# A selective-scan layer with experts on one core: the first half's out projection a state sooner, squares and norms in halves, the routing a state later

## The chip, the cores and the metric

The kernel runs on one core of a Trainium2 chip. The metric is the device time of one execution in microseconds (us), lower is better. The kernel before took 688.85 us (median of 3 runs, 685.72 to 689.6).

## The reference

The input is x of 4 sequences (batches) of 512 tokens, 128 wide. The program computes four residual steps; the change is in the first:

```
x = x + attn_a(layernorm(x))     # mamba block, then 8 experts, top 2
x = x + ffn(layernorm(x))
x = x + attn_b(layernorm(x))     # latent attention
x = x + ffn(layernorm(x))

attn_a(h0):
  h = rmsnorm(h0, w1);  xi, z = split(h @ in_proj)
  xi = silu(conv4(xi) + b)
  dbc = xi @ x_proj
  delta = softplus(dbc[:64] @ dt_proj + dt_b);  B = dbc[64:80];  C = dbc[80:96]
  for each of the 16 states n, over the 512 tokens t (256 channels):
     state_n[t] = exp(delta[t] * A_n) * state_n[t-1] + delta[t] * xi[t] * B_n[t]
     y[t] += state_n[t] * C_n[t]
  y = (y + D_skip * xi) * silu(z)
  r = h0 + y @ out_proj
  h2 = rmsnorm(r, w2)
  out = r + sum over the top 2 experts of weight * expert(h2)   # softmax of h2 @ router_w
```

## The kernel before, in words

Channels lie on the 128 partitions, so the 256 channels make two halves e = 0, 1, and tokens run along the free axis. One "state" g = 16 * b + n is state n of batch b; there are 64. `HB` = 2 batches make a half of the program: states 0 to 31 are the first half, states 32 to 63 the second; `first_1` = 32.

For each state five queues work:

- ScalarE (ACT): `decay(g, e)`, exp(delta * A_n) into PSUM (L1225). For states summed by VectorE it also copies the row of C into PSUM, `copy_c` (L1206), after the second decay. Further pieces of work are hung on (state, half) pairs by the table `COPY_AT` and run behind that decay: rows copied for the B and C store (`rows`, L1074), the softplus as `abs`, `relu`, `exp`, `log` (L1181, L1185, L1197, L1199), `squares` of r with their sums (L1068), `norm` (L1060), `input` (L1034), `logits` (L1048), `exps` (L1053). `c_by_token` (L1210) copies the turned C in state 35.
- GpSimd (POOL): the product delta * xi * B for both halves, called the B product here (L926, semaphore `dBx_ready`), into a ring of 3; for some states also the product of the scanned state with C, the C product (L935), two states later; the power for the second norm (`ROUTE_AT["power"]`, L887 and L888); `form_dx` (L914); and from state `SCATTER_FROM` = 48 on one of 16 scatters per state (`scatter`, L899), which put the first half's tokens into expert order.
- VectorE (DVE): the two scans of a state (L1574), for some states the weighing with C (L1586), `form_delta` (L1532), the gate of a finished batch (L1595), the residual additions (L1537), and the routing `top_a`, `top_b`, `find_slots` (L1446 to L1493).
- TensorE (PE): sums the weighed states with identity matmuls (`ysum`), projects ahead for the second half by the table `AHEAD`, runs `out_proj(0)` in state 34 ahead of that state's sums, and `turn_c` (L1953) in state 33, which turns the B and C rows for the states that are summed by token ("turned").
- SyncE (SP) issues the DMAs in program order: B row of state g (`spread_b`, L715), C row of state g - 2 (`spread_c`, L727), each spread to 128 partitions from a store in DRAM, and from state 36 on one of the 16 expert weights per state (L710). The first weight waits at L708 for `c_rows_turned`, since the weights land on memory that the first half used.

The order on each engine is written out by hand by these tables, and each queue runs in order. What the change touches is `AHEAD`, `COPY_AT`, `DELTA_AT`, `ROUTE_AT` and `SCATTER_FROM`, and the two helpers `norm_h2` and `squares`. What holds a queue shows in these lines:

```
if m == 0:                       # expert_weights, SyncE, state 36
    ...
    sp.wait_ge(s_ct, 1)
...
if AHEAD.get(g, ("",))[0] == "out_proj":    # PE, ahead of the sums
    ahead(*AHEAD[g])
...
sum_up(g - 1)
...
if g == TOKENS_AT:               # state 33
    turn_c()
...
if g == TOKENS_AT + 2:           # ACT, state 35
    c_by_token()
```

Of the kernel before, what the change touches and what calls it, by code (L numbers as in the profile page):

```python
# [36 lines left out]
def build(nc, x_in, rms1_w, rms2_w, in_proj_w, conv_w, conv_b, x_proj_w, dt_proj_w, dt_proj_b,  # L37
# [4 lines left out]
    TB = L // P  # L42
# [12 lines left out]
    HB = 2  # L55
# [9 lines left out]
    with ctx:  # L65
# [469 lines left out]
        for src, dst in ((0, wgT), (1, wuT), (2, None)):  # L535
            for t in range(HT):
# [18 lines left out]
                 16: ("taps", 1, 1), 18: ("taps1", 1, 0), 19: ("taps1", 1, 1), 22: ("x_proj", 0, 0), 24: ("dt_proj", 0, 0),  # L555
                 28: ("x_proj", 1, 0), 30: ("dt_proj", 1, 0), first_1 + 2: ("out_proj", 0, 0), 58: ("z", 1, 0), 61: ("z", 1, 1)}
        COPY_AT = {(5, 1): ("xi", 0, 0), (7, 1): ("xi", 0, 1), (9, 1): ("xi", 1, 0), (10, 1): ("xi", 1, 1),
                   (12, 1): ("conv", 0, 0), (13, 1): ("z", 0, 0), (15, 1): ("conv", 0, 1), (16, 1): ("z", 0, 1),
                   (21, 1): ("silu", 0, 0), (24, 1): ("rows", 0, 0), (26, 0): ("abs", 0, 0), (26, 1): ("relu", 0, 0),
                   (27, 0): ("abs", 0, 1), (27, 1): ("relu", 0, 1), (28, 0): ("exp", 0, 0), (29, 0): ("log", 0, 0),  # L560
                   (30, 1): ("rows", 1, 0), (32, 0): ("abs", 1, 0), (32, 1): ("relu", 1, 0), (33, 0): ("abs", 1, 1),
                   (33, 1): ("relu", 1, 1), (34, 0): ("exp", 1, 0), (35, 0): ("log", 1, 0),
                   (36, 0): ("squares", 0, 0), (36, 1): ("squares", 1, 0), (38, 0): ("norm", 0, 0), (38, 1): ("norm", 1, 0),
                   (40, 1): ("input", 0, 0), (41, 0): ("input", 1, 0), (43, 0): ("logits", 0, 0), (45, 0): ("exps", 0, 0),
                   (60, 1): ("z", 1, 0)}
        SILU_AT = 21
        XI_BANK, Z_BANK = ((5, 5), (5, 4)), ((4, 4), (4, 4))
        DELTA_AT = {4: 1, 30: 2, 36: 3}
        RESIDUAL_AT = first_1 + 3
        ROUTE_AT = {"power": first_1 + 6, "h2turn": first_1 + 7, "router": first_1 + 9,  # L570
                    "top_a": first_1 + 11, "top_b": first_1 + 13, "rank": first_1 + 14, "slots": first_1 + 15}
        TOKENS_AT = first_1 + 1
        SCATTER_FROM = first_1 + 16

# [438 lines left out]
        def _(act):  # L1013
# [40 lines left out]

            def norm_h2(c):

                act.wait_ge(s_rstd, 3)
                for j in range(TB):
                    t = TB * c + j
                    last = S.activation(nb[:, c, j, :], r[:, t, :], ACT.Copy, scale=small[:, 2, t:t + 1])  # L1060
                last.then_inc(s_h2, 1)

            def squares(c):

                act.wait_ge(s_r, c + 1)
                for j in range(TB):
                    t = TB * c + j
                    last = S.activation(nb[:, c, j, :], r[:, t, :], ACT.Square, accum_out=small[:, 3, t:t + 1])  # L1068
                if c == HB - 1:
                    last.then_inc(s_var, 1)  # L1070
# [90 lines left out]
            def copy_ahead(what, c, e):  # L1161
# [22 lines left out]
                elif what == "relu":  # L1184
                    S.activation(zr[:, e, L:HL], bank(DT[HB + c] + e), ACT.Relu, bias=dtb[:, e:e + 1]).then_inc(s_dtr, 1)  # L1185
                elif what == "squares":
                    squares(c)
                elif what == "norm":
                    norm_h2(c)
                elif what == "input":  # L1190
                    moe_input(c)
                elif what == "logits":
                    logits(0)
                elif what == "exps":
                    router_exp(0)
                elif what == "exp":
                    ch.link(S.activation(xT[:, :, :], xT[:, :, :], ACT.Exp, scale=-1.0))  # L1197
                elif what == "log":
                    S.activation(xT[:, :, :], xT[:, :, :], ACT.Ln, bias=1.0).then_inc(s_u, 1)  # L1199
# [1064 lines left out]
```

## Time and profile before

| | value |
|---|---|
| median of 3 runs | 688.85 us (685.72 to 689.6) |
| the profiled execution | 688.8 us, its span 687.0 us |
| PE busy | 570.7 us (83%) |
| VectorE busy | 475.6 us (69%) |
| ScalarE busy | 400.9 us (58%) |
| GpSimd busy | 324.6 us (47%) |
| scan, VectorE L1574 | 128 times, mean 1210 ns |
| B product, GpSimd L926 | 64 times, mean 2016 ns |
| C product, GpSimd L935 | 18 times, mean 2418 ns |
| decay, ScalarE L1225 | 128 times, mean 689 ns |
| chain that ended last | PE 36%, VectorE 9%, issue 7%, ScalarE 4%, GpSimd 3% |

The busy shares are averages over stages that have different limits. The states 0 to 63 run up to about 270 us; expert blocks, attention and feed-forward follow. What a change in one stage is worth is read from the timeline of that stage: each engine's rows in order of time, with the idle time before a row and what released it. Times in the rows count from the start of the span. In a matmul row one fp32 matmul stands as two records.

### The profile page before, as it was taken

What the parts mean: (1) busy time and instruction counts of PE and PEld (TensorE: products, weight loads), DVE (VectorE), ACT (ScalarE), POOL (GpSimd) and SP (SyncE); (2) the same over time, 40 slices, a digit from 0 to 9 for tenths busy, and PEclk for the clock granted to TensorE, in tenths of its full rate; (3) what the DMA queues carried; (4) which work ended last, traced back from release to release, by engine and by line L of the source; (5) the groups of instructions that cost most, each with busy time, mean ns of one, the idle gap of its engine ahead of it and who ended that gap; (6) DMA issues with size and microseconds to landing.
All of it is one profiled execution on the core that took longest, in us unless ns stands there. A gap on an engine that the chain in (4) does not pass through costs nothing.

```text
span 687.0 us, 11539 instructions
## 1 busy us (share of the span) xinstructions
PE 570.7 (83%) x3652; PEld 379.7 (55%) x3671; DVE 475.6 (69%) x1266; ACT 400.9 (58%) x666; POOL 324.6 (47%) x285
## 2 busy tenths in 40 slices
PE   2967899678677887889989999757799989988887
PEld 1423343224254564879989899625545545544466
DVE  4759997998789987536335653587777878886052
ACT  2677657756755776556756656314356556656731
POOL 5259988895996994225785324412011112112010
PEclk9979999899897999999999999957999999999999
DMA  5845455443755453201152003232003003000001
GB/s 142 305 167 159 150 186 154 143 129 109 241 183 160 142 135 100 68 16 36 54 133 86 20 17 105 68 100 58 9 25 87 10 20 92 4 3 3 1 16 47
DMA packets 49085, 63.32 MB, mean 92 GB/s; under 512 B 7570, under 2 KB 29090, under 8 KB 48770
## 3 DMA queue, kind: packets, MB, share of 16 engines
q1 hardware_dynamic: 43682, 56.65, 27.5%
q0 software_dynamic: 2496, 5.15, 2.1%
q10 hardware_dynamic: 2848, 0.78, 0.5%
q8 instruction: 31, 0.51, 0.3%
q14 instruction: 28, 0.23, 0.1%
HBM read 44.84 MB, written 9.52 MB: 79 GB/s over the span
## 4 chain that ended last, share of the span: by engine, by line
PE 36%; DVE 9%; issue 7%; ACT 4%; POOL 3%; DMA 1%; ACTq 1%; POOLq 0%; another core or an unknown queue 0%; DVEq 0%
PE ps L1792 33%; DVE arena L1712 3%; ACT arena L1296 2%; POOL moe_rows L899 1%; DVE stats L1383 1%; PE ps L2153 1%; DVE x L1647 1%; POOL moe_out L907 1%; DVE nb L1396 1%; ACT r L1296 1%; DMA moe_out<-arena,xT 1%; PE ps L2160 1%; ACT arena L1316 1%; ACT arena L1304 1%; ACTq L1286 1%
## 5 line engine op out<-in xcount | busy, mean ns | idle before, releaser
L1792 PE MATMUL ps<-arena 128*128 128x128 f32 (+11 forms) x2147 | 329.2, 329 | 42.9 <-DVE arena L1712 17.9
L1792 PEld LDWEIGHTS ps<-arena 128*128 128x128 f32 (+2 forms) x2166 | 209.0, 157 | 130.2 <-issue 59.3
L1574 DVE TENSOR_TENSOR_SCAN arena<-ps,arena 128x512 f32<-128x512 f32 x128 | 149.8, 1210 | 21.4 <-ACT ps L1225 15.2
L926 POOL TENSOR_TENSOR arena<-arena 128x1024 f32<-128x1024 f32 x64 | 127.9, 2016 | 25.5 <-DVE arena L1561 19.8
L1792 PE MATMUL ps<-arena,ident 128*128 128x512 f32 x216 | 109.5, 644 | 30.9 <-DVE arena L1586 30.8
L1712 DVE CUSTOM_DVE_ANT_0 arena<-ps,cmask 128x128 f32<-128x128 f32 (+3 forms) x256 | 111.5, 488 | 26.4 <-PE ps L1792 25.2
L1225 ACT ACTIVATE ps<-arena 128x512 f32<-128x512 f32 x128 | 87.4, 689 | 47.2 <-DVE arena L1574 45.5
L1792 PEld LDWEIGHTS ps<-arena,ident 128*128 128x128 f32 x216 | 42.4, 207 | 85.9 <-issue 44.2
L1296 ACT ACTIVATE arena<-ps 128x1024 f32<-128x1024 f32 (+3 forms) x86 | 57.0, 709 | 38.0 <-PE ps L1792 37.6
L907 POOL DMA_INDIRECT moe_out<-arena,xT x46 | 44.9, 976 | 66.5 <-DVE arena L1736 57.1
L1766 DVE TENSOR_TENSOR arena<-arena,ps 128x512 f32<-128x512 f32 x46 | 31.6, 688 | 57.1 <-PE ps L1792 43.6
L1343 ACT COPY arena<-arena 128x1024 f32 x46 | 48.2, 1048 | 13.9 <-issue 13.9
L871 POOL TENSOR_TENSOR small<-small,neghalf 128x4 f32<-128x4 f32 (+1 forms) x13 | 14.0, 1074 | 89.2 <-DVE small L1663 73.8
L935 POOL TENSOR_TENSOR arena<-arena 128x1024 f32<-128x1024 f32 x18 | 43.5, 2418 | 14.2 <-DVE arena L1574 13.1
L1353 ACT ACTIVATE arena<-ps 128x512 f32<-128x512 f32 x52 | 31.1, 598 | 24.4 <-PE ps L1792 22.3
L1586 DVE TENSOR_TENSOR arena<-arena,ps 128x1024 f32<-128x1024 f32 x36 | 43.1, 1198 | 0.2
L899 POOL DMA_INDIRECT moe_rows<-nb,xT x32 | 32.3, 1008 | 15.6 <-DVE xT L1493 8.6
L968 POOL TENSOR_TENSOR x<-x,arena 128x128 f32<-128x128 f32 x16 | 7.4, 460 | 67.4 <-DVE arena L1725 67.2
L1296 ACT ACTIVATE r<-ps 128x512 f32<-128x512 f32 (+3 forms) x42 | 27.8, 701 | 16.9 <-PE ps L1792 16.5
L1792 PE MATMUL ps<-kmask,identb 128*128 128x128 bf16 x256 | 35.1, 219 | 0.0
L1746 DVE TENSOR_TENSOR arena<-arena,ps 128x512 f32<-128x512 f32 x18 | 12.3, 686 | 28.7 <-ACT arena L1316 28.5
L1792 PEld LDWEIGHTS ps<-kmask,identb 128*128 128x128 bf16 x256 | 23.7, 98 | 12.4
(220 smaller groups left out, 700.3 us busy)
## 6 DMA issues: line engine op xcount, KB each, us to landing
arena<-bc_rows SPq DMA_DIRECT2D x118, 256.0 KB, 3.7
arena<-arena SPq DMA_DIRECT2D x64, 64.0 KB
arena<-arena SPq DMA_DIRECT2D x28, 128.0 KB, 2.4
moe_rows<-arena SPq DMA_DIRECT2D x2, 1495.0 KB, 11.8
arena<-moe_rows SPq DMA_DIRECT2D x8, 325.0 KB, 4.3
arena<-in_L_attn_a_Wg SPq DMA_DIRECT2D x8, 256.0 KB, 4.2
arena<-in_L_attn_a_Wu SPq DMA_DIRECT2D x8, 256.0 KB, 4.8
arena<-moe_out SPq DMA_DIRECT2D x4, 512.0 KB, 4.5
```

Of the source, the lines that this page charges most:

```text
L899: G.indirect_dma_start(moe_rows[h], bass.IndirectOffsetOnAxis(ap=slotu[:, h, k, t:t + 1], axis=0), nbr[:, t // TB, t % TB, :], None).then_ ...
L907: G.indirect_dma_start(moe_out[h], bass.IndirectOffsetOnAxis(ap=target[:, h, k:k + 1], axis=0), yb[:, i % YR, :], None).then_inc(s_yst[i % ...
L926: G.tensor_tensor(dBx[:, g % RING, :, :], dx[:, :, cs], bs[:, g % BS, :].unsqueeze(1).to_broadcast([P, CT, L]), ALU.mult).then_inc(s_dbx, 1)
L935: G.tensor_tensor(hC[:, slot(p), :, :], hst[:, p % STATES, :, :], cs_rows[:, row_slot(p), :].unsqueeze(1).to_broadcast([P, CT, L]), ALU.mu ...
L1225: S.activation(bank(6 + e), delta[:, e, c * L:c * L + L], ACT.Exp, scale=aneg[:, e, n:n + 1]).then_inc(s_da, 1)
L1296: S.activation(pts[c % 3][:, 2 * q:2 * q + 2, kt * P:L], ps[:, 2 * q:2 * q + 2, kt * P:L], ACT.Exp).then_inc(s_ex, 1)
L1343: S.copy(wst[:, i % 2, :, :].rearrange("p g f -> p (g f)"), wgu[:, bass.ds(expert, 1), :, :].rearrange("p o g f -> p (o g f)")).then_inc(s ...
L1574: V.tensor_tensor_scan(hst[:, g % STATES, e, :], bank(6 + e), dBx[:, g % RING, e, :], 0.0, ALU.mult, ALU.add).then_inc(s_scan, 1)
L1586: V.tensor_tensor(hC[:, slot(g), :, :], hst[:, g % STATES, :, :], bank(c_bank(g)).unsqueeze(1).to_broadcast([P, CT, L]), ALU.mult).then_in ...
L1712: last = V.tensor_tensor_reduce(out=junk[:, m % 2, col:col + w], in0=ps[:, 4 + m % 2, col:col + w], in1=cmask[:, L - w:L], scale=-1.0, sca ...
L1766: V.tensor_tensor(hs[:, i % 2, :], sg[:, m % 2, :], bank(2 + m % 2), ALU.mult).then_inc(s_hm, 1)
L1792: return T.matmul(o, l, rr, start=start, stop=stop)
```

## The change

The out projection of the first half runs on PE in state 33 rather than 34. The last batch's softplus runs on ScalarE a state sooner (`rows` at state 29 ... `log` at 34), but `form_delta(3)` on VectorE goes from state 36 to 38. `squares` and `norm` take half a batch (two tiles of 128 tokens) at a time, in four places each rather than two: squares in states 36 and 37, norms in 39 and 40 (before: 36, and 38). The power, the turn of h2, the router, `top_a`, `top_b`, the ranks and the slots, and the first scatter, all come one state later. No instruction is added or removed but the split of the loops.

```diff
-                 28: ("x_proj", 1, 0), 30: ("dt_proj", 1, 0), first_1 + 2: ("out_proj", 0, 0), 58: ("z", 1, 0), 61: ("z", 1, 1)}
+                 28: ("x_proj", 1, 0), 30: ("dt_proj", 1, 0), first_1 + 1: ("out_proj", 0, 0), 58: ("z", 1, 0), 61: ("z", 1, 1)}
...
-                   (30, 1): ("rows", 1, 0), (32, 0): ("abs", 1, 0), (32, 1): ("relu", 1, 0), (33, 0): ("abs", 1, 1),
-                   (33, 1): ("relu", 1, 1), (34, 0): ("exp", 1, 0), (35, 0): ("log", 1, 0),
-                   (36, 0): ("squares", 0, 0), (36, 1): ("squares", 1, 0), (38, 0): ("norm", 0, 0), (38, 1): ("norm", 1, 0),
-                   (40, 1): ("input", 0, 0), (41, 0): ("input", 1, 0), (43, 0): ("logits", 0, 0), (45, 0): ("exps", 0, 0),
+                   (29, 1): ("rows", 1, 0), (31, 0): ("abs", 1, 0), (31, 1): ("relu", 1, 0), (32, 0): ("abs", 1, 1),
+                   (32, 1): ("relu", 1, 1), (33, 0): ("exp", 1, 0), (34, 0): ("log", 1, 0),
+                   (36, 0): ("squares", 0, 0), (36, 1): ("squares", 0, 1), (37, 0): ("squares", 1, 0), (37, 1): ("squares", 1, 1),
+                   (39, 0): ("norm", 0, 0), (39, 1): ("norm", 0, 1), (40, 0): ("norm", 1, 0), (40, 1): ("norm", 1, 1),
+                   (41, 1): ("input", 0, 0), (42, 0): ("input", 1, 0), (43, 1): ("logits", 0, 0), (46, 0): ("exps", 0, 0),
...
-        DELTA_AT = {4: 1, 30: 2, 36: 3}
+        DELTA_AT = {4: 1, 30: 2, 38: 3}
...
-        ROUTE_AT = {"power": first_1 + 6, "h2turn": first_1 + 7, "router": first_1 + 9,
-                    "top_a": first_1 + 11, "top_b": first_1 + 13, "rank": first_1 + 14, "slots": first_1 + 15}
+        ROUTE_AT = {"power": first_1 + 7, "h2turn": first_1 + 8, "router": first_1 + 10,
+                    "top_a": first_1 + 12, "top_b": first_1 + 14, "rank": first_1 + 15, "slots": first_1 + 16}
...
-        SCATTER_FROM = first_1 + 16
+        SCATTER_FROM = first_1 + 17
...
-            def squares(c):
+            def squares(c, half):
...
-                for j in range(TB):
+                for j in range(2 * half, 2 * half + 2):
...
-                if c == HB - 1:
+                if half and c == HB - 1:
                     last.then_inc(s_var, 1)
```

`norm_h2` is cut in the same way; its semaphore is raised in the second half alone.

How the order of instructions moves is shown at three places. First PE in state 33, the turn of the C rows (L1953, `turn_c`) and the out projection (the rows 128x128). Before:

```order
L1792 MATMUL ps<-arena 128x512 [waits y_gated]
L1792 MATMUL ps<-arena 128x512
L1792 MATMUL ps<-arena,ident 128x512 [waits hC_ready]
L1792 MATMUL ps<-arena,ident 128x512
L1953 MATMUL ps<-ident,arena 128x32 [waits hC_ready,dt_ready]
L1953 MATMUL ps<-ident,arena 128x32 x7
L1792 MATMUL ps<-arena 128x128 [waits y_gated,dt_product_read]
L1792 MATMUL ps<-arena 128x128 x15
```

and with the change:

```order
L1794 MATMUL ps<-arena 128x512 [waits y_gated]
L1794 MATMUL ps<-arena 128x512
L1794 MATMUL ps<-arena 128x128 [waits y_gated,dt_product_read]
L1794 MATMUL ps<-arena 128x128 x15
L1794 MATMUL ps<-arena,ident 128x512 [waits hC_ready]
L1794 MATMUL ps<-arena,ident 128x512
L1955 MATMUL ps<-ident,arena 128x32 [waits hC_ready,dt_ready]
L1955 MATMUL ps<-ident,arena 128x32 x7
```

The out projection has moved ahead of the sum of state 32 and of the turn of the C rows.

Second ScalarE from the copy of the turned C (state 35) to the first decay of state 38. L1225 are the decays, L1206 the copies of a C row, L1068 the squares. Before:

```order
L1210 COPY arena<-ps 128x256 [waits c_rows_turned]
L1225 ACTIVATE ps<-arena 128x512 [waits scan_done]
L1068 ACTIVATE nb,small<-r 128x128 [waits residual_ready]
L1068 ACTIVATE nb,small<-r 128x128 x3
L1225 ACTIVATE ps<-arena 128x512 [waits scan_done]
L1206 COPY ps<-arena 128x512 [waits hC_ready,c_row_spread0]
L1068 ACTIVATE nb,small<-r 128x128 [waits residual_ready]
L1068 ACTIVATE nb,small<-r 128x128 x3
L1225 ACTIVATE ps<-arena 128x512 [waits scan_done] x2
L1206 COPY ps<-arena 128x512 [waits hC_ready,c_row_spread1]
L1225 ACTIVATE ps<-arena 128x512 [waits scan_done]
```

and with the change:

```order
L1212 COPY arena<-ps 128x256 [waits c_rows_turned]
L1227 ACTIVATE ps<-arena 128x512 [waits scan_done]
L1070 ACTIVATE nb,small<-r 128x128 [waits residual_ready]
L1070 ACTIVATE nb,small<-r 128x128
L1227 ACTIVATE ps<-arena 128x512 [waits scan_done]
L1208 COPY ps<-arena 128x512 [waits hC_ready,c_row_spread0]
L1070 ACTIVATE nb,small<-r 128x128 [waits residual_ready]
L1070 ACTIVATE nb,small<-r 128x128
L1227 ACTIVATE ps<-arena 128x512 [waits scan_done]
L1070 ACTIVATE nb,small<-r 128x128 [waits residual_ready]
L1070 ACTIVATE nb,small<-r 128x128
```

followed by

```order
L1227 ACTIVATE ps<-arena 128x512 [waits scan_done]
L1208 COPY ps<-arena 128x512 [waits hC_ready,c_row_spread1]
L1070 ACTIVATE nb,small<-r 128x128 [waits residual_ready]
L1070 ACTIVATE nb,small<-r 128x128
L1227 ACTIVATE ps<-arena 128x512 [waits scan_done] x3
```

The squares are spread over four places; the last two now stand between the copy of C row 37 and the decay of state 38.

Third VectorE from the second scan of state 36 on, with `form_delta(3)` (L1532). Before:

```order
L1574 SCALAR_TENSOR_TENSOR arena<-ps,arena 128x512 [waits dA_ready]
L1532 TENSOR_TENSOR arena<-arena,xT 128x2x512 [waits softplus_log_ready]
L1574 SCALAR_TENSOR_TENSOR arena<-ps,arena 128x512 [waits hC_ready,dBx_ready,dA_ready]
L1586 TENSOR_TENSOR arena<-arena,ps 128x1024 [waits y_summed,scan_done,c_row_copied]
L1574 SCALAR_TENSOR_TENSOR arena<-ps,arena 128x512 [waits dA_ready]
```

and with the change, from the same scan:

```order
L1576 SCALAR_TENSOR_TENSOR arena<-ps,arena 128x512 [waits dA_ready]
L1576 SCALAR_TENSOR_TENSOR arena<-ps,arena 128x512 [waits hC_ready,dBx_ready,dA_ready]
L1588 TENSOR_TENSOR arena<-arena,ps 128x1024 [waits y_summed,scan_done,c_row_copied]
L1576 SCALAR_TENSOR_TENSOR arena<-ps,arena 128x512 [waits dA_ready]
L1576 SCALAR_TENSOR_TENSOR arena<-ps,arena 128x512 [waits hC_on_pool_ready,dBx_ready,dA_ready]
L1588 TENSOR_TENSOR arena<-arena,ps 128x1024 [waits y_summed,scan_done,c_row_copied]
L1576 SCALAR_TENSOR_TENSOR arena<-ps,arena 128x512 [waits dA_ready]
L1534 TENSOR_TENSOR arena<-arena,xT 128x2x512 [waits softplus_log_ready]
```

`form_delta(3)` stands two states further on, behind the second scan of state 38. (The rows name a scan SCALAR_TENSOR_TENSOR; the trace names it TENSOR_TENSOR_SCAN.)

## Rows read from the trace of the kernel before

**Rows 1.** Chain of waits, one piece of it (start, us, what)

```profile
276.18 0.11 PE ps L2032
```

**Rows 2.** Busy time of one stretch: PE, PEld, DVE, ACT, POOL, granted clock, DMA, GB/s

```profile
217.00:266.00 49.00, 40.86 (x222) 27.65 (x221) 44.39 (x40) 34.80 (x71) 46.05 (x31) 1.00 0.42 128
```

**Rows 3.** DVE by time: start, us, line, operation, [idle before <- releaser]

```profile
143.51 3.18 DVE L1532 TENSOR_TENSOR arena<-arena,xT 128x1024 f32<-128x1024 f32 x1
...
167.08 0.69 DVE L1537 TENSOR_TENSOR r<-ps,r 128x512 f32<-128x512 f32 x1 [2.50 <-PE ps L1792]
...
169.47 2.33 DVE L1574 TENSOR_TENSOR_SCAN arena<-ps,arena 128x512 f32<-128x512 f32 x2
...
171.72 1.20 DVE L1532 TENSOR_TENSOR arena<-arena,xT 128x1024 f32<-128x1024 f32 x1
...
176.07 1.22 DVE L1574 TENSOR_TENSOR_SCAN arena<-ps,arena 128x512 f32<-128x512 f32 x1 [3.15 <-ACT ps L1225]
...
179.74 1.22 DVE L1574 TENSOR_TENSOR_SCAN arena<-ps,arena 128x512 f32<-128x512 f32 x1 [0.20 <-ACT ps L1225]
...
202.51 1.22 DVE L1574 TENSOR_TENSOR_SCAN arena<-ps,arena 128x512 f32<-128x512 f32 x1 [2.03 <-issue]
...
216.52 0.17 DVE L1493 CAST xT<-xT 128x16 uint32<-128x16 f32 x1
```

**Rows 4.** PE by time

```profile
161.58 2.87 PE L1792 MATMUL ps<-arena,ident 128*128 128x512 f32 x4
...
164.38 0.68 PE L1953 MATMUL ps<-ident,arena 32*128 32x32 f32 x8
...
164.99 3.84 PE L1792 MATMUL ps<-arena 128*128 128x128 f32 x32
...
168.66 3.60 PE L1792 MATMUL ps<-arena,ident 128*128 128x512 f32 x8
...
209.68 1.94 PE L1967 MATMUL ps<-ident,arena 128*128 128x128 f32 x8 [7.31 <-DVE arena L1574]
```

**Rows 5.** One microsecond, 163 to 164; columns as in rows 2

```profile
163.00:164.00 1.00, 1.00 (x3) 0.33 (x1) 1.00 (x2) 0.60 (x2) 1.00 (x1) 0.72 0.00 0
```

**Rows 6.** Waits of SyncE's DMA queue (us in total, times, longest)

```profile
SPq L708 <- PE ps L1953: 11.0, 1, 11.0
```

**Rows 7.** DMA issues of SyncE's queue by time

```profile
167.44 0.43 SPq L727 DMA_DIRECT2D arena<-bc_rows  x1
```

**Rows 8.** The source line L727 (C rows), 150 to 182 us

```profile
DMA to landing us min/median/max: 3.5/4.4/6.7
```

**Rows 9.** ACT by time

```profile
165.09 0.37 ACT L1210 COPY arena<-ps 128x256 f32<-128x256 f32 x1 [1.50 <-PE ps L1953]
...
173.66 0.59 ACT L1206 COPY ps<-arena 128x512 f32<-128x512 f32 x1 [4.00 <-DMA arena<-bc_rows]
...
174.18 0.30 ACT L1068 ACTIVATE nb<-r 128x128 f32<-128x128 f32 x1
...
175.36 1.28 ACT L1225 ACTIVATE ps<-arena 128x512 f32<-128x512 f32 x2
```

**Rows 10.** POOL by time, up to 225 us

```profile
169.74 2.00 POOL L926 TENSOR_TENSOR arena<-arena 128x1024 f32<-128x1024 f32 x1 [5.16 <-DMA arena<-bc_rows]
...
171.69 3.43 POOL L935 TENSOR_TENSOR arena<-arena 128x1024 f32<-128x1024 f32 x1
...
189.56 2.36 POOL L935 TENSOR_TENSOR arena<-arena 128x1024 f32<-128x1024 f32 x1
```

**Rows 11.** POOL by time, from 217 us

```profile
217.00 1.23 POOL L899 DMA_INDIRECT moe_rows<-nb,xT  x1 [6.42 <-DVE xT L1493]
...
263.27 2.01 POOL L926 TENSOR_TENSOR arena<-arena 128x1024 f32<-128x1024 f32 x1
```

**Rows 12.** SyncE's queue by time, from 262 us

```profile
267.79 11.81 SPq L757 DMA_DIRECT2D arena<-moe_rows  x5
```

More of the change, by code:

```diff
@@ L1053, in router_exp, with norm_h2 @@
                 S.activation(wtok[:, tiles_of(h), :], wtok[:, tiles_of(h), :], ACT.Exp).then_inc(s_re, 1)
-            def norm_h2(c):
+            def norm_h2(c, half):
                 act.wait_ge(s_rstd, 3)
-                for j in range(TB):
+                for j in range(2 * half, 2 * half + 2):
                     t = TB * c + j
                     last = S.activation(nb[:, c, j, :], r[:, t, :], ACT.Copy, scale=small[:, 2, t:t + 1])
-                last.then_inc(s_h2, 1)
-            def squares(c):
+                if half:
+                    last.then_inc(s_h2, 1)
+            def squares(c, half):
                 act.wait_ge(s_r, c + 1)
-                for j in range(TB):
+                for j in range(2 * half, 2 * half + 2):
                     t = TB * c + j
                     last = S.activation(nb[:, c, j, :], r[:, t, :], ACT.Square, accum_out=small[:, 3, t:t + 1])
-                if c == HB - 1:
+                if half and c == HB - 1:
                     last.then_inc(s_var, 1)
@@ L1186, in copy_ahead @@
                 elif what == "squares":
-                    squares(c)
+                    squares(c, e)
                 elif what == "norm":
-                    norm_h2(c)
+                    norm_h2(c, e)
                 elif what == "input":
```

## The prediction, made before the changed kernel ran

> **What bounds the kernel now.** I read the chain of waits first. It shows pieces only from 268 us on, and there it is serial: last sums, gate, second out projection, and the turn of the first expert block at 276.18 [rows 1]. So whatever the end of the scans loses or wins is passed on to the end of the kernel. Then the busy time by stretch, to see who paces the scans. From 217 to 266 us POOL is busy 46.05 of 49 us [rows 2]. Its own timeline says the same: from the first scatter at 217.00 to the product with B of state 63 that ends at 265.28 it repeats a scatter and a product, 16 scatters and 15 products, 15 steps of 3.21 us and a start of its own [rows 11]. VectorE is not the limit there; it is the end of `find_slots` at 216.69 [rows 3] that starts this row of work. So the question is what the change does to the time at which the slots are ready, and how much POOL has done by then.
>
> Between 159 and 217 us I followed VectorE's timeline for its holes. There are four that count [rows 3]: 2.50 us before the first residual addition at 167.08 (it waits for the out projection), 3.15 us before the scan of state 37 at 176.07, 0.20 us before state 38, and 2.03 us before state 45 at 202.51. The second is the one to understand. The scan waits for a decay of ScalarE at 175.36, which stands behind the second batch's four squares (from 174.18) and the copy of C row 36 at 173.66, and that copy waited 4.00 us for a DMA [rows 9]. The row was issued only at 167.44 [rows 7]. It was late because SyncE's queue stood still for 11.0 us at L708, the first expert weight, until PE had turned the C rows at L1953 [rows 6]. POOL felt it as well: its product for state 37 waited 5.16 us for a B row [rows 10]. So the turn of the C rows (`turn_c`, at 164.38 [rows 4]) is what releases the row traffic.
>
> **The change, part by part.**
>
> *Out projection ahead.* On PE it moves from behind `turn_c` to ahead of the sum of state 32. It starts at 161.58 instead of 164.99 [rows 4]. PE is then at half clock: in 163 to 164 us the granted clock averages 0.72 [rows 5], so 0.56 us of it were at 1.2 GHz (0.5 x 0.56 + 0.44 = 0.72) and 2.4 GHz came back at 163.56. A 128x128 record costs (168.66 - 164.99)/32 = 0.115 us at full clock and about 1.94/8 = 0.24 at 1.2 GHz [rows 4]. Of the 32 records some 8 run in the slow 2.0 us, the other 24 take 2.8, so it ends at 166.3. The sum of state 32 follows with four records of 0.43 (eight took 3.60 [rows 4]), 1.7 us, and `turn_c` starts at 168.0, **3.6 us later**. Bounds: all at full clock, 161.58 + 3.7 + 1.7 = 167.0 (+2.6); all at half clock, 161.58 + 7.7 + 2.9 = 172.1 (+7.7). I take 3.6, since the clock's history up to 161.58 is unchanged.
>
> *What it gives.* The 2.50 us hole before 167.08 closes. But ScalarE's copy of the turned C (at 165.09, behind a wait for L1953 [rows 9]) now comes at 168.7, and the decay of state 36 stands behind it. The scan of state 36 therefore starts at about 169.6, where it started at 169.47 [rows 3]. The gain is zero.
>
> *What it costs.* SyncE is released 3.6 us later, and issues the same transfers in the same order. C row 36 lands at 177.2 instead of 173.66, B row 37 at 173.3. ScalarE's copy, two squares (half of the 1.18 us from 174.18 to 175.36 [rows 9]) and the decay follow, so the scan of state 37 starts 3.6 - 0.6 = 3.0 us later, at 179.1. The 0.6 comes back at once: the last two squares now stand between the copy of C row 37 and the decay of state 38. State 38 is **+3.6 us**, at 183.3.
>
> *Last softplus a state sooner.* All of it sits on ScalarE before 163 us beside scans that don't wait for it; `abs` at state 31 stands behind `form_delta` (ends 146.69 [rows 3]) and still ahead of the decay that needs the scan of state 30. Its cover is that wait. The last `relu`, which the out projection waits for, comes before the gate that it waits for too. 0 us.
>
> *`form_delta(3)` from state 36 to 38.* It took 1.20 us at 171.72 [rows 3], inside the hole that ended at 176.07, so it was free. Behind the second scan of state 38 nothing hides it: **+1.1 us** for VectorE. At the same moment POOL starts the C product of state 38. When the two met at 171.7, POOL's product took 3.43 us against 2.36 alone [rows 10], so POOL pays 1.07 too. It has the slack of a wait for the scan of state 40 for part of it: the C product of state 40, at 189.56 before, comes at 194.1, **+4.5 us** in all (VectorE alone would make it +4.0).
>
> Which side pays depends on who is first. In the other order VectorE paid: 3.18 us at 143.51 [rows 3], 2.0 us more than 1.20, which would make the scan of state 40 5.9 us late.
> The Trainium skill, page "SBUF — State Buffer", section "Who interferes with whom", has it that a VectorE instruction with two SBUF inputs and a GpSimd instruction that reads SBUF exclude each other, the first to issue holding the shared ports to its end; that rule speaks against this move, which takes `form_delta` to where a product starts, and the trace shows both orders of it.
>
> *Norms and power.* POOL's power (about 1.9 us) moves behind the product of state 39. It starts when the last square is read, about 182.7, and the B product of state 40 ends about 186.6, just as the scan of state 38 does: no cost, but without margin. The norms end in state 40, and PE turns them then; nobody waits on PE.
>
> *To state 45.* From the C product of state 40 on, POOL was busy without a hole up to the scan of state 45: 202.51 - 189.56 = 12.95 us [rows 3, 10], and the change adds nothing to POOL there. State 45 comes at 207.0, still +4.5. The first routing piece (2 us) moves into the wait before it, which gives nothing, as it is POOL that ends that wait.
>
> *Routing a state later.* The slots now end after two more scans and one weighing: 3 x 1.12 = 3.4 us. In return POOL makes the product of state 49 before it waits for the slots, and so has one step of 3.21 us less to do after them [rows 11]. Net +0.2. One scatter more stands behind the last product. The gathered rows, loaded from 267.79 [rows 12], would be asked for at 273.5, and PE needs them at 280.9 (276.18 + 4.7); landing takes about 4 us by the nearest row I have (3.5 to 6.7 [rows 8]), so it stays hidden.
>
> **Sum.** +4.5 + 0.2 = +4.7 us on the profiled execution's 688.8, **693.5 us**. The median of the three runs shown is 688.85, so the two bases agree.
>
> **The rivals.** A measurement of this kernel can tell about 0.5% (3.4 us) from no change.
>
> (A) *The row comes faster.* C row 36 took 6.2 us from issue to use; other C rows landed after 4.4, at best 3.5 [rows 8]. If the shifted transfers meet less traffic and the row lands after 3.5, the copy starts at 174.5, +0.9, and the end is +0.9 + 0.9 + 0.2, about 690.8 us: not slower. Against it: the same ten transfers are issued within the same 5 us, so they crowd each other as before. It decides from a landing under 4.9 us.
>
> (B) *Half clock.* If PE stays at 1.2 GHz through the out projection, `turn_c` is 7.7 us late rather than 3.6, and the time is 697.6. For it: that half clock ended at 163.56 just as the work changed; against it: PE is busy without a hole in both.
>
> (C) *VectorE loses the port*, see above: 5.9 + 0.2, 694.9 us.
>
> (D) *Nothing is late.* If the rows did not hang on `turn_c`, the holes of 2.50 and 3.15 would both close; with 0.6 for the squares before state 38, 1.1 for `form_delta` and 0.2 behind, -5.65 + 1.9 = -3.7, 685.1 us. The 11.0 us at L708 [rows 6] speaks against it.
>
> **How the numbers follow.** The forecast 0.55, A 0.20, B 0.08, C 0.09, D 0.05, and 0.03 for the change having no effect at all. Slower by over 0.5% are B, C and most of the forecast's own spread (692 to 695; a tenth falls under 692.3): 0.66. Faster is D with a little of A: 0.06. The same takes the rest, 0.28. The range of 8 in 10 goes from 688.5, inside A, to 696.5, between C and B; the forecast's own bounds are 692.0 (both lock costs gone, `turn_c` at +2.6) and 695.
>
> **What would show it.** Right, if in the new profile `turn_c` starts at about 168 behind the out projection; L708 waits 14 to 15 us; the copy of C row 36 starts near 177; a hole of about 2.6 us stands before state 36 and one of about 7 us before the scan of state 37, near 179; `find_slots` ends near 224.5; and the last scan starts near 270.5. The hole before the residual addition gone, and the one before state 37 more than twice its 3.15 us, is the mark of the mechanism. Wrong, if the copy of row 36 starts before 175 (A), or if the time from state 38 to the slots is not that of before.

## The result, and the profile after

| | before | after |
|---|---|---|
| median | 688.67 us (685.72 to 689.6, 4 runs) | 694.36 us (693.61 to 696.57, 4 runs) |
| the profiled execution | 688.8 us, span 687.0 us | 693.63 us, span 691.9 us |
| first gate to third gate, VectorE | 157.78 to 272.85: 115.07 us | 158.76 to 276.71: 117.95 us |
| third gate to the end of the span | 414.15 us | 415.19 us |

The kernel became slower: ratio 1.0089, interval [1.0056, 1.0122], in microseconds +3.9 to +8.4. But for the softplus of the last batch, all that the change moves lies between the gate of batch 1 and the gate of batch 3 (L1595 before, L1597 after; the first and the third gate from 150 us on, and so called below). The third line of the table is where its effect must be read. There the profiled execution lost 2.9 us, less than the medians say; why is answered below. The profiled execution after reaches its first gate 0.98 us later than that of before; these 0.98 us are there in full at the first scan of state 28 already (136.81 and 137.79), ahead of everything that the change moves. Wherever times of two executions are compared, they are therefore counted from the first gate.

The rows of after follow the order of the prediction. PE by time (start, us, line, operation; the 36 records at 160.03 are 4 of the skip product and the 32 of the out projection):

```profile
160.03 5.55 PE L1794 MATMUL ps<-arena 128*128 128x512 f32 x36 [1.83 <-DVE arena L1597]
...
165.43 1.89 PE L1794 MATMUL ps<-arena,ident 128*128 128x512 f32 x4
...
167.24 0.68 PE L1955 MATMUL ps<-ident,arena 32*128 32x32 f32 x8
```

The turn of the C rows (L1955) has moved behind the out projection and the sum of state 32. It starts 8.48 us after the first gate, before 6.60 [rows 4]: 1.88 us later. SyncE's wait at the first expert weight grew with it, from 11.0 us [rows 6] to 12.9:

```profile
SPq L709 <- PE ps L1955: 12.9, 1, 12.9
```

SyncE's queue by time: the queue starts again 0.8 us behind the turn, and C row 36 is issued 2.3 us later, as before in the same order (167.44 there [rows 7]):

```profile
168.01 0.34 SPq L711 DMA_DIRECT2D arena<-in_L_attn_a_Wg  x1
...
170.29 0.43 SPq L728 DMA_DIRECT2D arena<-bc_rows  x1
```

ScalarE by time, for [rows 9]:

```profile
167.95 0.37 ACT L1212 COPY arena<-ps 128x256 f32<-128x256 f32 x1 [3.89 <-PE ps L1955]
...
176.37 0.59 ACT L1208 COPY ps<-arena 128x512 f32<-128x512 f32 x1 [6.27 <-DMA arena<-bc_rows]
...
176.90 0.30 ACT L1070 ACTIVATE nb<-r 128x128 f32<-128x128 f32 x1
...
177.49 0.67 ACT L1227 ACTIVATE ps<-arena 128x512 f32<-128x512 f32 x1
...
181.14 0.30 ACT L1070 ACTIVATE nb<-r 128x128 f32<-128x128 f32 x1
```

The copy of the turned C waits 3.89 us for PE, and the copy of C row 36 waits 6.27 us for its DMA (before: 1.50 and 4.00). Row 36 is used 6.08 us after its issue, before 6.22 [rows 7, 9]: it did not come faster, it was asked for later. VectorE by time, for [rows 3]:

```profile
158.76 1.22 DVE L1597 TENSOR_TENSOR arena<-ps,arena 128x1024 f32<-128x1024 f32 x1
...
165.48 0.69 DVE L1539 TENSOR_TENSOR r<-ps,r 128x512 f32<-128x512 f32 x1
...
167.21 0.67 DVE L1539 TENSOR_TENSOR r<-ps,r 128x512 f32<-128x512 f32 x1
...
168.95 2.41 DVE L1576 TENSOR_TENSOR_SCAN arena<-ps,arena 128x512 f32<-128x512 f32 x2 [1.07 <-ACT ps L1227]
...
178.19 1.22 DVE L1576 TENSOR_TENSOR_SCAN arena<-ps,arena 128x512 f32<-128x512 f32 x1 [6.83 <-ACT ps L1227]
...
182.44 1.22 DVE L1576 TENSOR_TENSOR_SCAN arena<-ps,arena 128x512 f32<-128x512 f32 x1 [0.78 <-ACT ps L1227]
...
185.83 1.20 DVE L1534 TENSOR_TENSOR arena<-arena,xT 128x1024 f32<-128x1024 f32 x1
...
206.05 3.45 DVE L1576 TENSOR_TENSOR_SCAN arena<-ps,arena 128x512 f32<-128x512 f32 x3 [1.96 <-POOL arena L927]
...
223.67 0.17 DVE L1495 CAST xT<-xT 128x16 uint32<-128x16 f32 x1
...
269.68 1.23 DVE L1576 TENSOR_TENSOR_SCAN arena<-ps,arena 128x512 f32<-128x512 f32 x1 [0.20 <-ACT ps L1227]
...
276.71 1.22 DVE L1597 TENSOR_TENSOR arena<-ps,arena 128x1024 f32<-128x1024 f32 x1 [2.25 <-PE ps L1794]
```

The hole of 2.50 us before the first residual addition is gone, the one before the scan of state 37 has grown from 3.15 to 6.83 us, a hole of 1.07 us stands before state 36, and `form_delta(3)` sits at 185.83 with no idle time around it. Last GpSimd by time, for [rows 10, 11]:

```profile
172.59 2.00 POOL L927 TENSOR_TENSOR arena<-arena 128x1024 f32<-128x1024 f32 x1 [7.04 <-DMA arena<-bc_rows]
...
181.92 0.19 POOL L888 TENSOR_SCALAR small<-small 128x8 f32<-128x8 f32 x1 [1.13 <-ACT nb L1070]
...
186.04 3.20 POOL L936 TENSOR_TENSOR arena<-arena 128x1024 f32<-128x1024 f32 x1 [0.25 <-DVE arena L1576]
...
193.12 2.36 POOL L936 TENSOR_TENSOR arena<-arena 128x1024 f32<-128x1024 f32 x1
...
224.15 1.23 POOL L900 DMA_INDIRECT moe_rows<-nb,xT  x1 [7.82 <-DVE xT L1495]
...
267.12 2.01 POOL L927 TENSOR_TENSOR arena<-arena 128x1024 f32<-128x1024 f32 x1
```

The B product of state 37 waits 7.04 us for its row (before 5.16). The product of state 38 starts 0.21 us behind `form_delta` and takes 3.20 us where one alone takes 2.36. The first scatter comes at 224.15 with 14 products behind it where before had 15 [rows 11], and the last of them ends at 269.1.

One thing was not expected. These are two windows of before, from 160 us on (PE, weight load, VectorE, ScalarE, GpSimd busy; granted clock; DMA share; GB/s):

```profile
160.00:162.00 2.00, 2.00 (x4) 0.86 (x3) 2.00 (x3) 1.78 (x4) 1.74 (x1) 0.54 0.00 0
162.00:164.00 2.00, 2.00 (x4) 0.66 (x2) 2.00 (x3) 1.60 (x3) 2.00 (x2) 0.61 0.00 0
```

and the same of after:

```profile
160.00:162.00 2.00, 1.97 (x6) 1.01 (x7) 2.00 (x2) 0.86 (x2) 0.76 (x1) 1.00 0.00 0
162.00:164.00 2.00, 2.00 (x21) 2.00 (x20) 2.00 (x3) 1.59 (x3) 2.00 (x2) 1.00 0.00 0
```

Before ran here at 1.2 GHz for most of the time, after at 2.4 GHz throughout. The out projection, which the prediction had start at half clock, ran at full clock.

### The profile page after: what moved, and what is told of

Read it like the earlier page. It is cut to its first block, busy times and chain, and to the rows that moved or that the text cites. A ratio compares the mean times of both kernels' runs of the same rounds, so it can differ in the third digit from the quotient of the medians.

```text
span 691.9 us, 11558 instructions
## 1 busy us (share of the span) xinstructions
PE 574.8 (83%) x3671; PEld 380.5 (55%) x3671; DVE 475.3 (69%) x1266; ACT 400.2 (58%) x666; POOL 323.9 (47%) x285
## 4 chain that ended last, share of the span: by engine, by line
PE 36%; DVE 9%; issue 7%; ACT 4%; POOL 3%; DMA 1%; ACTq 1%; POOLq 0%; DVEq 0%
PE ps L1794 33%; DVE arena L1714 3%; ACT arena L1298 2%; POOL moe_rows L900 1%; DVE stats L1385 1%; PE ps L2155 1%; DVE x L1649 1%; POOL moe_out L908 1%; DVE nb L1398 1%; PE ps L2162 1%; DMA moe_out<-arena,xT 1%; ACT arena L1318 1%; ACTq L1288 1%; DVE mv L1388 0%; ACT arena L1306 0%
## 5 line engine op out<-in xcount | busy, mean ns | idle before, releaser
L1794 PE MATMUL ps<-arena 128*128 128x128 f32 (+11 forms) x2166 | 333.0, 329 | 44.2 <-DVE arena L1714 17.9
L1576 DVE TENSOR_TENSOR_SCAN arena<-ps,arena 128x512 f32<-128x512 f32 x128 | 150.0, 1210 | 27.3 <-ACT ps L1227 21.3
L1208 ACT COPY ps<-arena 128x512 f32<-128x512 f32 x36 | 20.9, 580 | 17.0 <-DMA arena<-bc_rows 10.0
```

Of the source, the lines that this page charges most:

```text
L1576: V.tensor_tensor_scan(hst[:, g % STATES, e, :], bank(6 + e), dBx[:, g % RING, e, :], 0.0, ALU.mult, ALU.add).then_inc(s_scan, 1)
L1794: return T.matmul(o, l, rr, start=start, stop=stop)
```

## The experiments

Ten kernels ran, in three groups, each group on one chip together with the kernel before. On the chip of the first and third group every kernel takes some 11 us more (before: 699.57 and 700.46 us), on that of the second group before took 689.03 us. Ratios are always to the runs of before on the same chip.

All readings of the profiled executions stand in one table; times in us from the first gate (VectorE L1595, with the change L1597). "Clock" is PE's level there: half where the two windows above average 0.50 to 0.59 and 0.55 to 0.97, full where both are 1.00. "Slots" is the start of `find_slots`' last instruction.

| kernel | clock | first gate at | turn of C | copy of C row 36 | slots | third gate |
|---|---|---|---|---|---|---|
| before | half | 157.78 | 6.60 | 15.88 | 58.74 | 115.07 |
| after | full | 158.76 | 8.48 | 17.61 | 64.91 | 117.95 |
| after, again | full | 158.57 | 8.48 | 17.65 | 65.00 | 118.11 |
| out projection only | full | 158.10 | 8.49 | 17.49 | 60.34 | 116.59 |
| all but the out projection | full | 159.58 | 4.91 | 14.64 | 61.97 | 115.08 |
| turn early in before | half | 158.01 | -0.75 | 11.02 | 56.23 | 112.56 |
| turn early in after | half | 157.39 | -0.80 | 9.56 | 58.24 | 111.29 |
| `form_delta` at 38 only | half | 156.52 | 6.60 | 16.09 | 59.80 | 116.12 |
| after, `form_delta` at 36 | half | 157.37 | 10.14 | 18.97 | 65.46 | 118.57 |
| out projection and turn early | half | 156.67 | -0.90 | 9.34 | 54.65 | 110.89 |
| routing only | half | 156.78 | 6.60 | 15.37 | 61.84 | 114.88 |
| turn early, `form_delta` at 36 | full | 158.29 | -0.62 | 9.24 | 58.68 | 111.77 |

### The out projection alone, and all but it

The first kernel is before with only this:

```diff
-  first_1 + 2: ("out_proj", 0, 0)
+  first_1 + 1: ("out_proj", 0, 0)
```

> The kernel before with the out projection alone moved to state 33. Theory (the turn of the C rows stands behind it and holds the row traffic): the turn starts 1.9 us (full clock, as in the profile of the change) to 3.6 us (half clock first) later, L708 waits 13 to 15 us, the scan of state 37 and all behind it come 1.9 to 3.6 us later, so the ratio to before is 1.003 to 1.005. Rival (it is the rest of the change that costs, and the earlier out projection gives 2.5 us by the hole before the residual addition): 0.996 to 0.999.

Measured: 702.98 us against 699.57, ratio 1.0064 [1.0044, 1.0084], a little above the 1.003 to 1.005 that was expected. The turn stood 8.49 us behind the gate, and SyncE waited 12.9 us at the first weight. The second is after with the same line put back:

```diff
-  first_1 + 1: ("out_proj", 0, 0)
+  first_1 + 2: ("out_proj", 0, 0)
```

> The changed kernel with the out projection put back to state 34: squares and norms in halves, softplus sooner, form_delta at 38, routing later. Theory: the C row of state 36 is copied near 173.7 as before, the halves of the squares cancel, form_delta costs about 1 us and the routing 0.2, ratio to before 1.001 to 1.003. Rival (the rest is what costs): 1.006 or more.

Measured: 700.88 us, ratio 1.0019 [1.0002, 1.0035]. So the loss is in the out projection's move, and the rest costs a little: added, the two ratios give 1.0083. VectorE of the second kernel, for the two holes in question:

```profile
167.18 0.69 DVE L1539 TENSOR_TENSOR r<-ps,r 128x512 f32<-128x512 f32 x1 [0.79 <-PE ps L1794]
...
176.04 1.22 DVE L1576 TENSOR_TENSOR_SCAN arena<-ps,arena 128x512 f32<-128x512 f32 x1 [4.14 <-ACT ps L1227]
```

With the out projection behind the turn, the hole before the residual addition is back (0.79 us at full clock, 2.50 at half), and that before state 37 is 4.14 us rather than 6.83. The second kernel and after ran at the same clock. From gate to gate they differ by 117.95 - 115.08 = 2.87 us, with the turn 8.48 - 4.91 = 3.57 us later. Most of the missing 0.7 us is the row: from the turn to the copy of C row 36 it took 17.61 - 8.48 = 9.13 us in after and 14.64 - 4.91 = 9.73 in the second kernel.

### The turn of the C rows ahead of it all

If everything hangs on when PE turns the C rows, then turning them a state sooner must win, whatever the out projection does. In before and in after:

```diff
-        TOKENS_AT = first_1 + 1
+        TOKENS_AT = first_1
```

> The kernel before with the turn of the C rows on PE in state 32 and its copy on ScalarE in state 34. Theory: SyncE is released near 157 instead of 165, no engine waits for a row in states 36 and 37, the hole of 3.15 us before the scan of state 37 goes and that of 2.50 stays, the scan of state 37 starts near 173, ratio to before 0.995 to 0.996. Rival (the row is late for its own traffic, not for SyncE's wait): the copy of C row 36 still starts after 172 and the ratio is 0.999 to 1.001.

Measured: 697.53 us, ratio 0.9974 [0.9959, 0.9989]: faster, by less than was expected. The hole before the residual addition stays (1.59 us), and `form_delta(3)` took 2.71 us beside a product of GpSimd.

> The changed kernel with the turn of the C rows in state 32 and its copy in state 34, so that the out projection has nothing of the row traffic behind it. Theory: the holes of 1.07 and 6.83 us before states 36 and 37 go, the scan of state 37 starts near 170.5, ratio to before 0.995 to 0.998, some 7 to 8 us under the changed kernel, and near or under the kernel with the early turn alone. Rival (the change costs by other parts): ratio to before over 1.000.

Measured: 695.82 us, ratio 0.9955 [0.994, 0.9971], so it is faster than before while after is slower. No hole is left before states 36 and 37. From gate to gate the changed kernel falls from 117.95 us (full clock) to 111.29 us (half clock) by this one line. The two kernels with the early turn ran at the same level, and between them the rest of the change loses nothing any more: 111.29 us against 112.56. So what the change costs is not the work it moves but the turn that it delays.

### `form_delta` and its place

```diff
-        DELTA_AT = {4: 1, 30: 2, 36: 3}
+        DELTA_AT = {4: 1, 30: 2, 38: 3}
```

> The kernel before with form_delta of the last batch moved from state 36 to 38 alone. Theory: 1.0 to 1.2 us more on the way to the slots, gate to gate 116.1 us against 115.1, ratio 1.001 to 1.003. Rival (no cost): 0.999 to 1.001 and 115.1.

Measured, this line alone in before: 689.26 us against 689.03, ratio 1.0012 [0.9985, 1.0038]. The time does not tell it from nothing; from gate to gate, at the same clock as before, it is 116.12 - 115.07 = 1.05 us. Of these 16.09 - 15.88 = 0.21 us are a C row that came later, which leaves 0.84 us for `form_delta`. The opposite edit in after:

> The changed kernel with form_delta of the last batch back in state 36, inside the hole of 6.8 us. Theory (it costs where it was put, on VectorE and by GpSimd's product beside it): 1 to 2 us less than the changed kernel, ratio to before 1.004 to 1.007, gate to gate 116 to 117 us. Rival (GpSimd ends the later waits and has the slack): no difference from the changed kernel.

Measured: 692.95 us, ratio 1.0064 [1.0039, 1.0088]. From gate to gate it took 118.57 us and not the 116 to 117 expected, but at half clock, with the turn 10.14 - 8.48 = 1.66 us later than in after; less these it would be 116.9 us, an estimate. After itself ran beside it:

> The changed kernel as it is, once more beside before, on the chip of the runs it is compared with. If the parts add up, out projection (1.0064) and rest (1.0019) give 1.008; a ratio of 1.006 to 1.010 is expected. From gate to gate (start of the gate of batch 1 to that of batch 3) 117.9 us as in the first profile, against 115.1 before.

Measured: 693.53 us, ratio 1.0056 [1.003, 1.0083], just under the 1.006 to 1.010 expected, and 118.11 us from gate to gate. By the time the two can't be told apart. The first of them is worth more for another reason: it is the changed order of PE in an execution with half clock. PE by time:

```profile
158.65 7.22 PE L1794 MATMUL ps<-arena 128*128 128x512 f32 x36 [1.98 <-DVE arena L1597]
...
165.70 1.89 PE L1794 MATMUL ps<-arena,ident 128*128 128x512 f32 x4
...
167.51 0.68 PE L1955 MATMUL ps<-ident,arena 32*128 32x32 f32 x8
```

The same 36 records take 7.22 us here and 5.55 in after. VectorE of the same kernel:

```profile
169.22 2.41 DVE L1576 TENSOR_TENSOR_SCAN arena<-ps,arena 128x512 f32<-128x512 f32 x2 [2.63 <-ACT ps L1227]
...
171.55 1.20 DVE L1534 TENSOR_TENSOR arena<-arena,xT 128x1024 f32<-128x1024 f32 x1
...
178.16 1.22 DVE L1576 TENSOR_TENSOR_SCAN arena<-ps,arena 128x512 f32<-128x512 f32 x1 [5.41 <-ACT ps L1227]
```

The hole before state 36 is 2.63 us, as the prediction gave it (2.6), and 1.07 in after at full clock.

### The routing alone

This is before with the routing and the first scatter a state later, and with the pieces that stand between them on ScalarE; norms, squares, power, `form_delta` and the out projection stay:

```diff
-  (40, 1): ("input", 0, 0), (41, 0): ("input", 1, 0), (43, 0): ("logits", 0, 0), (45, 0): ("exps", 0, 0),
+  (41, 1): ("input", 0, 0), (42, 0): ("input", 1, 0), (43, 1): ("logits", 0, 0), (46, 0): ("exps", 0, 0),
...
-  ROUTE_AT = {"power": first_1 + 6, "h2turn": first_1 + 7, "router": first_1 + 9,
-              "top_a": first_1 + 11, "top_b": first_1 + 13, "rank": first_1 + 14, "slots": first_1 + 15}
+  ROUTE_AT = {"power": first_1 + 6, "h2turn": first_1 + 8, "router": first_1 + 10,
+              "top_a": first_1 + 12, "top_b": first_1 + 14, "rank": first_1 + 15, "slots": first_1 + 16}
...
-  SCATTER_FROM = first_1 + 16
+  SCATTER_FROM = first_1 + 17
```

> Only the routing of the kernel before goes a state later: the turn of h2, the router, top_a, top_b, the ranks and the slots, with the norms' inputs, logits and exps behind them, and the first scatter in state 49; the power stays in state 38, the out projection in 34, form_delta in 36. Theory (the term of the prediction): two scans and one weighing more stand ahead of the slots (+3.4 us), and GpSimd has one step of 3.21 us less to do after them, so from the first gate to the third it takes 115.1 to 115.6 us where the kernel before took 115.07 with its PE at half clock at the turn of the C rows; with PE at full clock there both are about 1.7 us less. Ratio to the kernel before 0.999 to 1.002. Rival: GpSimd's head start is lost again (it does not pace the states behind the slots by itself), then 118.3 us and 1.004 to 1.006. Second rival: the slots themselves come less than 3.4 us later because two holes of VectorE fill, then below 115 us.

Measured: 700.48 us against 700.46, ratio 0.9987 [0.9963, 1.0011], and 114.88 us from gate to gate, 0.2 less than before at the same clock. The slots are ready 61.84 - 58.74 = 3.10 us later, yet the third gate is not. C row 36 was in use 0.51 us sooner in this execution; without that the routing would cost 0.51 - 0.19 = 0.3 us, so the head start of GpSimd makes up for nearly all of the later slots, and the rival with 118.3 us is out. GpSimd of this kernel, first scatter and the product behind it:

```profile
219.10 1.23 POOL L899 DMA_INDIRECT moe_rows<-nb,xT  x1 [7.81 <-DVE xT L1493]
...
220.37 2.00 POOL L926 TENSOR_TENSOR arena<-arena 128x1024 f32<-128x1024 f32 x1
```

### A version that beats both

The out projection of the change, the turn a state sooner, and nothing else, in before:

```diff
-  first_1 + 2: ("out_proj", 0, 0)
+  first_1 + 1: ("out_proj", 0, 0)
...
-        TOKENS_AT = first_1 + 1
+        TOKENS_AT = first_1
```

> The kernel before with two edits: turn of the C rows in state 32 (copy in 34) and out projection in state 33. Theory: nothing hangs on the out projection then, so the hole of 2.50 us closes as well and it gains on the early turn alone (0.9974): ratio 0.993 to 0.996, gate to gate 110.5 to 112. Rival (GpSimd already ends every wait there): the same as the early turn alone, 0.996 to 0.998.

Measured: 683.86 us (681.18 to 686.11) against 689.03, ratio 0.9923 [0.9895, 0.9951]. This is the lowest ratio of all, clearly below the early turn alone (0.9974 [0.9959, 0.9989]); from the changed kernel with the early turn (0.9955 [0.994, 0.9971]) the times do not tell it apart. From gate to gate the three took 110.89, 112.56 and 111.29 us, all at half clock. So with the turn out of its way the earlier out projection wins 112.56 - 110.89 = 1.67 us. SyncE's wait at the first weight is down from 11.0 us to 3.5:

```profile
SPq L708 <- PE ps L1953: 3.5, 1, 3.5
```

PE by time, the turn ahead of the out projection, and this ahead of the sum of state 32:

```profile
155.77 0.68 PE L1953 MATMUL ps<-ident,arena 32*128 32x32 f32 x8
...
157.94 7.23 PE L1792 MATMUL ps<-arena 128*128 128x512 f32 x36 [1.49 <-DVE arena L1595]
...
165.01 5.33 PE L1792 MATMUL ps<-arena,ident 128*128 128x512 f32 x12
```

VectorE by time, where neither the residual additions nor the scans of states 36 and 37 stand behind idle time any more:

```profile
163.49 0.68 DVE L1537 TENSOR_TENSOR r<-ps,r 128x512 f32<-128x512 f32 x1
...
165.81 2.33 DVE L1574 TENSOR_TENSOR_SCAN arena<-ps,arena 128x512 f32<-128x512 f32 x2
...
168.06 2.44 DVE L1532 TENSOR_TENSOR arena<-arena,xT 128x1024 f32<-128x1024 f32 x1
...
170.42 1.21 DVE L1574 TENSOR_TENSOR_SCAN arena<-ps,arena 128x512 f32<-128x512 f32 x1
...
174.08 1.22 DVE L1574 TENSOR_TENSOR_SCAN arena<-ps,arena 128x512 f32<-128x512 f32 x1 [0.20 <-ACT ps L1225]
```

GpSimd of the same kernel, two products around `form_delta`:

```profile
167.06 2.36 POOL L935 TENSOR_TENSOR arena<-arena 128x1024 f32<-128x1024 f32 x1 [1.65 <-DVE arena L1574]
...
169.38 2.98 POOL L926 TENSOR_TENSOR arena<-arena 128x1024 f32<-128x1024 f32 x1
```

The last experiment asks whether `form_delta` still wants its place in state 36 once the holes are gone. It is after with both `TOKENS_AT = first_1` and `DELTA_AT = {4: 1, 30: 2, 36: 3}`.

> The changed kernel with the turn of the C rows in state 32 and form_delta(3) back in state 36. With the rows early there is no hole in front of states 36 and 37 any more that could hide form_delta, so the theory says that its place is worth nothing now: gate to gate 111.0 to 112.0 us, where the version with form_delta in state 38 took 111.29, and a ratio to the kernel before of 0.991 to 0.996. Rival: GpSimd's product is what form_delta meets in either state, and state 36 is the worse or the better place by more than 1 us; then gate to gate lies outside 110.3 to 112.3.

Measured: 697.26 us against 700.46, ratio 0.9943 [0.9914, 0.9972], and 111.77 us from gate to gate, within the 111.0 to 112.0 expected, where state 38 gave 111.29. The two ran at different levels of the clock, so these times don't settle half a microsecond, but no effect of the place shows beyond that: there is no hole to hide it in.

## Why the prediction was right, and where it was right by less than it seems

The forecast was 693.5 us, and 694.36 was measured. That the profiled execution came to 693.63, closer still, is luck. Of its 4.9 us of longer span 0.98 arose ahead of the change, 2.88 between the gates, and 1.04 behind the third gate; there after's own two profiles differ by 4.3 us (415.2 and 410.9 to the end of the span). The mechanism of the forecast was the one that happened, and each mark that it named is in the rows of after but for their size. By its own steps:

**The hole that closes gives nothing.** Right. The residual additions start with no idle time in front, and the scan of state 36 waits for ScalarE instead. Counted from the gate it starts at 10.19 us, before at 169.47 - 157.78 = 11.69, but these 1.5 us are the clock: at full clock all but the out projection has it at 9.99, and at half clock after with `form_delta` at 36 has it at 11.85. At equal clock it comes 0.2 us later in both pairs, where 0.13 was forecast.

**`turn_c` 3.6 us later.** Right at equal clock, wrong between the two executions. At full clock it went from 4.91 (all but the out projection) to 8.48, +3.57; at half clock from 6.60 (before) to 10.14 (after with `form_delta` at 36), +3.54. But the profiled execution of after was at the other level than that of before, and so showed +1.88. The step that failed is the sentence "the clock's history up to 161.58 is unchanged": the code ahead is unchanged but for ScalarE's pieces, the level is not. The bounds failed for the same reason: the lower one, +2.6, put the out projection at full clock and left the skip product ahead of it at half.

**The row traffic, states 37 and 38.** The forecast had the copy of row 36 at 177.2, the scan of state 37 at 179.1 and `find_slots` done near 224.5. From the gate that is 19.4, 21.3 and 66.7; measured were 17.6, 19.4 and 65.1. Each is early by 1.6 to 1.9 us, the amount by which `turn_c` is early. At half clock the copy came at 18.97 and the scan at 20.79. So this single term carries the whole difference between forecast and trace of 4.7 and 2.9 us. The wait at L709 was 12.9 rather than 14 to 15 us; at half clock it was 14.6.

**The last softplus a state sooner: no cost.** Right. From the first scan of state 31 to the first gate it took 10.03 or 10.04 us in all twelve profiles, with the old place and the new.

**`form_delta` +1.1 us, of it 0.9 us on GpSimd's path.** Right: +1.05 us from gate to gate alone in before, 0.84 without the later row. The C product of state 40 starts in after at 193.12 - 158.76 = 34.36 us from the gate, before at 31.78, or 30.1 at full clock (an estimate, see below): +4.3 us, forecast +4.5. The order of the two was the one taken for the sum too: VectorE came first and took 1.20 us, the product of state 38 3.20 us.

**Routing later, +0.2 us net.** Right within what can be seen (-0.2 us, or +0.3 without the row that came 0.5 us sooner). The gathered rows loaded behind the last scatter stayed hidden: from the third gate to the first turn of the expert block it takes 3.2 us in both.

**Squares, norms, power: no cost.** Close. All but the out projection costs 115.08 us at full clock. Before was profiled only at half clock; less the 1.69 us by which its turn was late for that (6.60 - 4.91), it would take 113.4, an estimate. Of the difference of 1.7 us `form_delta` makes 0.84 and the routing 0.3. A further 0.45 us is the C row, which came 9.73 us behind the turn there and 9.28 in before. The squares cancel as forecast: two less stand before state 37, and the hole before state 38 is 0.78 us rather than 0.20, since the last two stand in front of its decay. About 0.1 us is left.

At equal clock the sum is thus 117.95 - 113.4 = +4.6 us at full clock, and at half clock 118.57 + 0.84 - 115.07 = +4.3 us (the 0.84 for `form_delta`), where +4.7 was forecast. Both are estimates, since neither kernel was profiled at the other's level. This is also what the timed runs say better than the pair of profiles does: +5.7 us of the medians of the first comparison and +4.5 us of the second. An effect of 2.9 us lies outside the interval of the first, one of 4.3 to 4.6 us inside both. The clock of the timed executions in this stretch was not recorded, so that they were mixed alike in both kernels is argued, not shown.

**The rivals.** (A), a row that comes faster, did not happen: from SyncE's release to the copy of row 36 it took 8.4 us in after, 8.5 before, and 8.0 to 9.0 in all executions with the turn in state 33. (B), half clock through the whole out projection, did not happen either: even in the execution that began it at half clock the row of 36 records took 7.22 us, 1.7 us more than at full clock, so 2.4 GHz came back within it. (C), VectorE losing the port at state 38, showed only in after with the turn early. At state 36 it lost it in all three other kernels with the early turn, and in the routing alone too, where `form_delta` took 3.18 us inside the hole. (D), nothing late, was wrong by its own condition, the 12.9 us at L709; with the turn early its number came out, 111.29 us from gate to gate, 3.8 us won over before, though `form_delta` lost the port there, which (D) did not have.

## What to carry to other kernels

When a queue in program order stands at a wait, ask what releases it before moving anything in front of the releaser: here 3.6 us of matmuls that nobody needed sooner were put ahead of eight small transposes that let all row traffic go, and one number that moved those transposes turned a loss of 0.6 to 0.9% into a gain of 0.5%. A hole that closes is worth nothing if the wait behind it has another cause, so follow the next waiting instruction before a gain is booked. And compare two profiles at equal clock, from a common event just ahead of the change, or a difference of 1.7 us that is not the change's is taken for it.

## What the runs showed of the hardware

**The same place runs at either clock.** The stretch of 1.2 GHz between 158 and 164 us is there in all seven executions whose first gate starts at 158.01 us or sooner, and in none of the five from 158.10 us on, whatever the kernel. Before and "all but the out projection" issue the same matmuls there, and their turn stands at 6.60 and 4.91 us from the gate; three kernels at half clock agree to 0.01 us on 6.60. After and after with `form_delta` at 36 issue the same instructions up to state 36, and one ran at full clock, the other at half: 5.55 and 7.22 us for the same 36 records. So executions can differ by 1.7 us here without any edit. Idle time of PE at the gate does not sort them either: it was 1.83 us in after, 1.98 in after with `form_delta` at 36, 1.49 in the kernel with out projection and turn early, and in before, by its PE row:

```profile
159.05 2.73 PE L1792 MATMUL ps<-arena 128*128 128x512 f32 x4 [1.95 <-DVE arena L1595]
```

What does sort them, besides the arrival, is the stretch of 1.2 GHz before this one, which all twelve have between 148 and 156 us. The gate starts 7.9 to 8.2 us behind the beginning of that stretch in the seven and 7.4 to 7.6 us in the five. The Trainium skill, page "TensorE: Matmul & The Clock Gate", Part 1, says that the gate's periods are "free-running" and don't start anew with the kernel. The trace agrees so far as the same instructions met either level; what set the arrival, which differed by up to 2.1 us at the first scan already (42.4 to 44.5 us), was not looked into.

**The port is held to the end of an instruction, and both sides can pay.** With the turn early, `form_delta` met two products. In the kernel with out projection and turn early it starts at 168.06, while a product runs to 169.42. It takes 2.44 us, which is the 1.36 us left of the product and 1.08 of its own, and the next product, at 169.38, takes 2.98 us rather than 2.0. The changed kernel with the turn early shows it again, VectorE:

```profile
176.41 2.57 DVE L1534 TENSOR_TENSOR arena<-arena,xT 128x1024 f32<-128x1024 f32 x1
```

and GpSimd:

```profile
175.90 2.00 POOL L927 TENSOR_TENSOR arena<-arena 128x1024 f32<-128x1024 f32 x1
...
177.85 3.33 POOL L936 TENSOR_TENSOR arena<-arena 128x1024 f32<-128x1024 f32 x1
```

1.49 us are left of the first product, and 2.57 - 1.49 = 1.08; the second takes 3.33 rather than 2.36. So one VectorE instruction of 1.20 us takes 1.2 to 1.4 us more on its own engine and makes the other's 1.0 us longer. This is the lock that the Trainium skill, page "SBUF — State Buffer", section "Who interferes with whom", describes; the trace agrees with it, and adds that an instruction which lost once wins the next time. The routing alone shows the same at state 36 (`form_delta` 3.18 us, the product behind it 2.97 rather than 2.0).

**One chip is slower behind the change, not in it.** From the third gate to the end of the span it took 411 to 416 us in the profiles of before, of after and of the second group, and 424 to 428 us in those of the first and third group. From gate to gate no such difference shows: after took 117.95 and 118.11 us, and its two halves, on the other chip, fit these by the sums above. What differs there was not looked into.
